# A recommendation network on one core: the first chunk's first cross layer in two halves of two tiles, with three tiles prepared ahead instead of four

## What is computed

```python
target = item_id_feat + item_img_feat
seq_emb = item_table[item_seq]                      # 2048 x 50 rows of 128
x = jnp.concatenate([t, seq_emb, t - seq_emb, t * seq_emb], axis=-1)
scores = (jax.nn.relu(x @ aw1 + ab1) @ aw2 + ab2)[..., 0]
weights = jax.nn.softmax(jnp.where(mask, -1000000000.0, scores), axis=1)
hist_feat = jnp.einsum('bs,bsd->bd', weights, seq_emb)
sparse = jnp.stack([like_feat, view_feat, item_id_feat, item_img_feat, hist_feat], axis=1)
se = sparse * w[:, :, None]                         # w: gate from the means of sparse
p = [vids[:, i] * se[:, j] for i in range(4) for j in range(i + 1, 5)]
dnn_in = jnp.concatenate([se.reshape(B, -1), bil.reshape(B, -1)], axis=1)   # 15 x 128
for i in range(2):
    xc = dnn_in * (xc @ cross_K[i] + cross_bias[i]) + xc
h = jax.nn.gelu(_ln(xc @ w1 + b1, ln1g, ln1b), approximate=False)
h = jax.nn.gelu(_ln(h @ w2 + b2, ln2g, ln2b), approximate=False)
return jax.nn.sigmoid(h @ w3 + b3)[:, 0]
```

## Time and profile before

| | us |
|---|---|
| median of 3 runs | 2186.22 |
| the three runs | 2185.83, 2186.22, 2200.5 |
| the profiled execution, its own time | 2193.55 |
| its span, first to last instruction | 2191.7 |
| mean granted TensorE clock | 0.920 of full speed |

### The profile page before, as it was taken

The page is one execution under the profiler, slowest core; times in us unless marked ns, Lnnn a source line. Parts: engine busy times, 40 slices in busy tenths (PEclk is TensorE's granted clock), DMA queues, the critical chain, the costliest instruction groups (busy, mean ns, idle before and its releaser), DMA issues. The chain is left out here.

```text
span 2191.7 us, 32802 instructions
## 1 busy us (share of the span) xinstructions
PE 1955.1 (89%) x9608; PEld 1534.4 (70%) x9608; DVE 1333.1 (61%) x2213; ACT 902.9 (41%) x1963; POOL 895.4 (41%) x854
## 2 busy tenths in 40 slices
PE   1655653999999999989999999999999999999997
PEld 1433432777777787777777887777777888888885
DVE  3444444567687766566777765667778755445553
ACT  1333333354444434655444434564445333322223
POOL 6666666565565540455555520546551000000000
PEclk6655555999999999999999999999999999999998
DMA  4111111334343463233343452334333352233330
GB/s 155 43 45 45 42 45 41 105 108 121 110 122 99 134 212 91 82 98 103 111 122 114 121 197 80 88 92 120 109 119 98 102 175 84 86 97 100 97 89 20
DMA packets 99535, 220.31 MB, mean 101 GB/s; under 512 B 21648, under 2 KB 27040, under 8 KB 99232
## 3 DMA queue, kind: packets, MB, share of 16 engines
q1 hardware_dynamic: 62928, 136.90, 20.6%
q0 software_dynamic: 27136, 55.63, 10.0%
q10 hardware_dynamic: 9296, 25.70, 3.1%
HBM read 205.29 MB, written 12.85 MB: 100 GB/s over the span
## 5 line engine op out<-in xcount | busy, mean ns | idle before, releaser
L388 POOL DMA_INDIRECT e<-in_item_table,idx_all x800 | 846.5, 1058 | 713.8 <-issue 332.2
L1081 DVE TENSOR_TENSOR Wl<-raw,Wh 128x640 fp32r<-128x640 f32 (+1 forms) x420 | 338.0, 805 | 298.8 <-DVEq L1080 254.7
L765 ACT ACTIVATE Wh<-raw 128x640 fp32r<-128x640 f32 (+1 forms) x420 | 301.7, 722 | 501.2 <-ACTq L764 438.7
L513 PE MATMUL xps<-X0h,Wh 128*128 128x512 f32 x900 | 366.1, 407 | 6.7 <-PEq L511 6.7
L513 PE MATMUL xps<-X1h,Wh 128*128 128x512 f32 x900 | 359.9, 400 | 0.0
L515 PE MATMUL xps<-X0h,Wl 128*128 128x512 f32 x900 | 353.1, 392 | 0.0
L514 PE MATMUL xps<-X0l,Wh 128*128 128x512 f32 x900 | 352.8, 392 | 0.0
L515 PE MATMUL xps<-X1h,Wl 128*128 128x512 f32 x900 | 351.7, 391 | 0.0
L514 PE MATMUL xps<-X1l,Wh 128*128 128x512 f32 x900 | 351.4, 390 | 0.0
L728 ACT ACTIVATE e<-e,pw 128x128 f32<-128x128 f32 x800 | 242.6, 388 | 15.4 <-ACTq L122 10.3
L430 PE MATMUL aps<-ident,e 128*128 128x128 f32 x700 | 113.0, 297 | 102.4 <-issue 83.4
(11 more groups left out here) (144 smaller groups left out, 2240.4 us busy)
## 6 DMA issues: line engine op xcount, KB each, us to landing
raw<-in_cross_K SPq DMA_DIRECT2D x360, 320.0 KB
raw<-in_w SPq DMA_DIRECT2D x60, 256.0 KB
e<-in_item_table,idx_all POOLq DMA_INDIRECT x800
dnn_scratch<-dn ACTq DMA_DIRECT2D x12, 960.0 KB
x1f<-dnn_scratch ACTq DMA_DIRECT2D x3, 2048.0 KB, 9.7
x1f<-dnn_scratch ACTq DMA_DIRECT2D x3, 1792.0 KB
dn<-in_embT SPq DMA_DIRECT2D x1, 1024.0 KB
img_scratch<-dn ACTq DMA_DIRECT2D x1, 1024.0 KB, 5.3
```

Source lines behind the costliest of these rows:

```text
L388: nc.gpsimd.indirect_dma_start(out=dst, out_offset=None, in_=table, in_offset=bass.IndirectOffsetOnAxis(ap=idx_all[:, t, s:s + 1], axis=0) ...
L513: m0 = mm(out, wh, Xh[:, 0:T, k, :], start=(k == 0), stop=False)
L765: af(Wh[:, split_slot(w), 0:n], raw[:, rs, 0:n], ACT.Copy).then_inc(hi_done, 1)
L1081: v.tensor_tensor(Wl[:, rs, 0:n], raw[:, rs, 0:n], Wh[:, slot, 0:n].bitcast(F32), ALU.subtract).then_inc(lo_done, 1)
```

## The change

The first chunk's layer 0 is run twice, once for its tiles 0 and 1 and once for 2 and 3, each time 15 half steps of 256 columns, with layer 0's 45 weight blocks streamed twice. The first half needs tiles 0 and 1 only, so the opening keeps the groups of three tiles (15, 18 steps), and tile 3's groups move under the half steps. In these a group stands in every second step, 15 in all (tiles 3, 4 and 5), its ten transposes come in one run into six places of the transposes' banks and four of the third product bank, which half steps leave, and its later parts are spread over four half steps. Layer 1 of chunk 0 has ten groups (tiles 6 and 7) in its first ten steps, the last in step 24 of 0 to 29. The wait after every five gathers begins at tile 3. Chunks 1 to 3 keep their plan.

```diff
-GROUP_STEPS = {
-    4: [[1 + 6 * j + g for g in range(NG)] for j in range(4)],
...
+EARLY = 2
+EXTRA = FEATS * UNITS
+LEAD = 3
+OPEN_TILES = 3
+OPEN_STEPS = LEAD + NG * OPEN_TILES
+EARLY_AT = OPEN_STEPS
+CHUNK_AT = EARLY_AT + FEATS
...
+    where = [[LEAD + NG * j + g for g in range(NG)] for j in range(OPEN_TILES)]
+
+    where += [[EARLY_AT + 2 * (NG * j + g) for g in range(NG)] for j in range(3)]
+    where += [[CHUNK_AT + FEATS + NG * j + g for g in range(NG)] for j in range(2)]
...
+            if plan[k].half:
+
+                opened = k + 2
+                scored = opened + 1 if plan[opened].half else opened
...
-                        if (s + 1) % (GRP if t < TILES[0] else SUB) == 0:
+                        if (s + 1) % (GRP if t < OPEN_TILES else SUB) == 0:
...
+            def transposes10(t, g, swing):
+                pe.wait_ge(e_landed[g], (t + 1) * (DMA * GRP))
+                pe.wait_ge(tp_free, 1).then_inc(tp_free, -1)
+                for i in range(GRP):
+                    out = tps6[:, i * P:(i + 1) * P] if i < 6 else tps4[:, (i - 6) * P:(i - 5) * P]
+                    last = nc.tensor.transpose(out, e_sub(g, i // SUB, i % SUB), ident[:])
...
+            def half_step(p):
+                products(p, 0)
+                if p.scored:
+                    score()
+                if p.open:
+                    hidden()
+                if p.lift is not None:
+                    tail_turn(p.lift)
+                if p.grp:
+                    transposes10(*p.grp, p.swing is not None)
+                if p.pair is not None:
+                    tail_bilinear()
+
+                products(p, 1)
+                products(p, 2)
+                if p.share is not None:
+                    head_share(p.share)
...
+            def half_step(p):
+                unit(p.first)
+                if p.fetch is not None:
+                    head_fetch(p.fetch)
+                if p.summed:
+                    exps(p.summed[1])
+                    weigh(p.summed[1])
+                unit(p.first + 1)
+                if p.prev:
+                    x_hi(p.prev)
+                unit(p.first + 2)
+                if p.gate is not None:
+                    tail_gate()
+                if p.spread is not None and p.spread < TILES[0]:
+                    tail_hi(p.spread)
+                elif p.spread is not None:
+                    tail_store(p.spread)
+                if p.lift is not None:
+                    tail_copy(p.lift)
+                if p.grp:
+                    copy_eT10(p.swing)
...
+                    if p.spread == TILES[0] - 1:
+                        dve.sem_inc(x_ready, FEATS)
```

More of the change, by code:

```diff
@@ L95, in make_plan @@
-    for c in range(1, CHUNKS):
-        at = open_steps + STEPS * (c - 1)
-        where += [[at + k for k in ks] for ks in GROUP_STEPS[TILES[c]]]
+    plan = [Step(None, k) for k in range(OPEN_STEPS)]
+    plan[-1].last = True
+    for k in range(FEATS):
+        plan.append(Step(0, k, (0, EARLY), k * UNITS))
+        plan[-1].early = True
+    for c in range(CHUNKS):
+        for k in range(STEPS):
+            tiles = (EARLY if c == 0 and k < FEATS else 0, TILES[c])
+            plan.append(Step(c, k, tiles, EXTRA + c * STREAM + k * UNITS))
@@ L98, in make_plan @@
+    for i, p in enumerate(plan[EARLY_AT:EARLY_AT + 2 * FEATS]):
+        p.half, p.bank = True, i % 2
+        p.to_bank2 = i == 2 * (FEATS - 1)
+    for p, q in zip(plan, plan[1:]):
+        if p.chunk is not None and q.chunk == p.chunk:
+            q.prev = p
+    where = group_steps()
+    assert len(where) == sum(TILES)
     for t, ks in enumerate(where):
         for g, k in enumerate(ks):
-            plan[k].grp = plan[k + 1].open = plan[k + 2].summed = (t, g)
-        s, last = ks[0], ks[-1]
@@ L102, in make_plan @@
-        if t < TILES[0]:
+            if plan[k].half:
+                opened = k + 2
+                scored = opened + 1 if plan[opened].half else opened
+            else:
+                opened = scored = k + 1
+                if plan[opened].half:
+                    scored = opened + 1
+                elif plan[opened].chunk is None and not plan[opened].last:
+                    scored = None
+            summed = k + 2 if scored is None else scored + 1
+            plan[k].grp = plan[k + 1 if plan[k].half else k].timed = (t, g)
@@ L627, in step @@
                     transposes(*p.grp, 0)
-                products(p.chunk, p.layer, p.n, 1)
+                products(p, 1)
                 if p.grp:
-                    transposes(*p.grp, 1)
+                    transposes(*p.grp, 1, p.swing is not None)
                 elif p.swing is not None:
@@ L639, in step @@
                     fc_w3(T)
-                products(p.chunk, p.layer, p.n, 2)
+                products(p, 2)
                 if T and 2 <= k < T + 2:
@@ L1207, in step @@
                 if prev:
[L1208 removed]
+                    x_sum(prev)
                 if p.summed:
```

310 lines of the change are left out of this document (200 added, 110 removed).

## The result

The changed kernel takes 2238.39 us (median of 4, 2236.76 to 2238.87), the kernel before 2188.2 us (median of 4, one more run than above): a ratio of 1.0216, 95% interval 1.0189 to 1.0243. It is slower by 1.9 to 2.4%, 48 us above the forecast of 2190 and outside its range. The profiled execution has a span of 2234.6 us against 2191.7.

What follows compares the result with a forecast made beforehand. GpSimd's gathers were taken to bound the first chunk to tile 7's end: 733.6 plus 65.3 us puts w1 at 798.9 instead of 795.30, +3.6 on the 2186.2 median, 2190 us; range 2168 to 2214.

Steps and rivals of the forecast that it cites:

- Step 3: TensorE up to tile 7's last group: half-step pairs of 15.6 us, done at 666, 68 us before the gather.
- the narrow product: Layer 0's 256-column matmuls on TensorE: pitch taken as 0.12 us, bounded by 0.11 and 0.227.
- step 4: VectorE and ScalarE in half steps: below 13 and 10 of 19.2 us; gate chains delay TensorE a few us per tile.
- Step 1: GpSimd's gathers, tiles 3 to 7: 50 sub-groups of five at 9.23 us plus feature triples, ending at 733.6, not 719.7.
- the 14.7: Tile 3's gathers with waits after five: 96.05 us instead of 81.35, +14.7.
- Step 2: From tile 7's last group to the w1 stage: one bare step fewer, 65.3 us, so w1 at 798.9, +3.6.
- Step 5: End of chunk 0: later row store and loads covered by weight blocks three ahead; counted 0, with 4 us as other end.
- The first product: Sign of being right, start of layer 0 on TensorE: near 256 instead of 382.
- C: TensorE falls behind, through narrow products at 0.227 us (2266) or a mean clock of 0.85 (ties with gathers); chance 0.05.
- Rival B: VectorE's two-input instructions lengthen GpSimd's gathers, a fifth of their time; up to 23 us more, 2213; chance 0.13.
- A: The opening's ten steps are really saved: w1 64 us earlier, 2122, or 2155 in part; chance 0.10.

Runs made afterwards that it cites:

- s5: Changed kernel plus idle identity transposes on TensorE ahead of the gate's transposes and the second half's first product; 2249.23 us, ratio 1.0234.
- s7: Changed kernel with VectorE subtracting only 384 of 640 columns of the half steps' weight blocks; half steps 331.8 us against 359.2.
- s6: Changed kernel with five slots instead of four for the weights' high parts, second head matrix kept at half width; half steps 359.6 us against 359.2.
- e3: Changed kernel with gate transposes and exponential later, the hidden layer's maximum and tile 3's pairs earlier on VectorE; 2227.89 us, ratio 1.0126.
- s9: Changed kernel with the edits of s7 and e3, and VectorE summing one row of ten for tiles 3 to 5; half steps 290.7 us.
- b1: Kernel before, waiting after five gathers instead of ten for tile 3 too; tile 4's gathers start 7.9 us later, w1 stage at 804.1.
- b2: Kernel before with one more two-input VectorE instruction ahead of each of layer 0's 45 weight subtractions; layer 0 goes from 211.5 to 225.1 us.

## Why the prediction was wrong, and where it was right

*Where the failure is.* Step 3 had TensorE arrive at tile 7's last group at 666 at the earliest, and put 68 us of slack between that and the gathers at 733.6. It arrived at 778.06: 112 us late, 68 of them covered, 44 not. 843.3 - 798.9 is 44.4. So the forecast had the wrong stream last: the gathers were to bind and TensorE to idle ahead of them, and TensorE came last, with GpSimd waiting for it. What follows tile 7's last group was right to 0.1 us.

*The term.* The pair of half steps: 15.6 us in step 3. From the first group's transposes at 275.93 to layer 1's first at 633.94 it is 358.0 us for 15 pairs, **23.9 each**, tails and the second half's start among them. That is 124 us more than 15 x 15.6; the group steps of layer 1 gave some 16 back against the 160 allowed for them and the tails (144.1 for the nine from 633.94 to 778.06), and the start was 4 late. Of the 124, 88 are TensorE's idle time, the rest is slower work at the granted 0.87 and what step 3 counted under tails; by s5 the slower work cost no time of its own. The part that was doubtful, the narrow product, was right: at full clock they start 0.12 us apart, as in these three rows:

```profile
281.75 0.28 PE L593 MATMUL xps<-X0h,Wh 128*128 128x256 f32 x1
281.87 0.28 PE L594 MATMUL xps<-X0l,Wh 128*128 128x256 f32 x1
281.99 0.28 PE L595 MATMUL xps<-X0h,Wl 128*128 128x256 f32 x1
```

*The step that let it through* is step 4. It put VectorE below 13 us of the 19.2 in which GpSimd delivers a group, and called the rest "a few us once per tile". Three errors are in it. It scaled busy time (10.4 us per step plus three blocks), where a half step also repeats each short instruction with its gap: 14.5 us busy and 3.9 of gaps in a pair, 18.4, which is all but the whole of 19.2. It took an engine at less than the period for harmless, although VectorE works its queue in order and each piece waits for TensorE or ScalarE somewhere. And it priced the chains (8.4 us at each gate, 11.3 and 5.4 at the halves' first products) as stalls that slack pays for, when the ordinary pairs were already longer than the gathers': 20.15 us even at full clock, 275.93 to 296.08. From one group's transposes to the next, ten of the 15 pairs took 20.1 to 23.9 us, 21.4 in the mean, and the five others 25.4 to 32.2; four of these hold a tile's gate or the second half's start. An estimate from these: with 21.4 in all 15, TensorE would have come to tile 7's last group near 741 (275.9 + 321 + 144.1), 7 us behind the gathers; the other 37 came with the five long pairs. s7 is the plainest test of VectorE's part: 24.7 us of subtractions less, 27.4 us less time, in the same order of work. What exactly closes the loop through VectorE's 72 us of longer waits was not singled out; that they are not for want of lead (s6) and only in part for the order (e3) is shown.

*Step 1* was near. In s9, where GpSimd waits for nobody, tile 3 takes 98.57 us beside the weight stream (113 GB/s), against 96.05 in the sum: 9.48 a sub-group. The 40 later ones take 9.27, and tile 7 is through at 737.28 instead of 733.6.

```profile
253.06:351.63 98.57, 76.66 (x548) 68.44 (x547) 57.00 (x110) 48.27 (x110) 56.84 (x53) 0.83 0.40 113
```

b1's +7.9 for the same waits is 8.57 a sub-group without the stream, where the kernel before had 8.54. So its shortfall does not speak against the 14.7. "GpSimd would feel such lag only if a buffer came back late" was right as a condition, and it came to pass: 72.1 us.

*Step 2* was exact for what it sized: 778.06 to 843.29 is 65.23 us, 65.3 predicted.

*Step 5*: the w1 stage takes 44.3 us from its first to its last product against 40.2 before. That is the size of the 4 us named as the other end and counted as 0, but not their cause. The store is issued at 844.85, 1.6 us into the stage as foreseen, the loads at 850.24, and no wait of TensorE follows them. Its one wait in the stage is ahead of them, for a product bank:

```profile
847.88 0.47 PE L624 MATMUL xps<-Wh,X0h 128*128 128x512 f32 x1 [2.14 <-PEq L617]
```

VectorE had tile 7's pairs to do from 842.83 and read the bank only at 846.83. The rest is slower products behind that wait, at a granted 0.96 over the stage.

*The first product* was to come near 256 and came at 268.84, because tile 1's rows are finished only in the last opening step (5.44 us of wait at L591). Group one's transposes were 4 us late for it.

*The rivals.* C was the case that came true, TensorE falls behind, but not by either of its two prices: the pitch is 0.12, and the clock's 0.87 lay above its 0.85 and cost nothing that s5 could show. It should have had a third entry, VectorE. Rival B (gathers lengthened by VectorE) has its piece in b2, some 2 us of longer instructions for 37 us of added work, and is not what happened. A needed 7.9 us per sub-group, and none measured here, with or without the weight stream, had a mean below 8.5. The Trainium skill, "SBUF — State Buffer", section "Who interferes with whom", has two-input VectorE instructions contend with GpSimd instructions that read SBUF; the same section says, as an inference, that making DMA descriptors needs the write side instead, for which such a VectorE instruction does not contend. Of 37 us added in b2 a twentieth shows in the gather instructions, which is nearer to the second; the fifth in rival B had only been read off beside it. The Trainium skill's warning in "TensorE: Matmul & The Clock Gate", section "HAM oscillation — how this bites in real kernels", was borne out as to the pattern (0.80 to 0.83 behind the long waits, 0.90 to 1.00 with the filler) and not as to the time.

No version beats the kernel before. e3 is the best one that computes everything, at 1.0126. Even s9, with work left out, starts its w1 stage 6.5 us later than before, because the gathers of tile 7 end at 737 there.

## What to carry to other kernels

When a step is cut into two, count for every engine the instructions that are repeated, with the gap in front of each, and not the busy time that is moved: VectorE, 64% busy in layer 0 before, came to 96% of the gathers' period that way. Slack pays for a stall only while no other engine is near the same period, as VectorE was here. And to find which engine sets the pace of a loop in which all of them wait, take some 30 us from each in turn; the waits of the trace named TensorE's suppliers, but taking 17 us of those waits away gave 1 us, while 25 to 28 us less work on VectorE gave 20 to 27.

## What the runs showed of the hardware

- Fewer waits for landing made the kernel slower: with one after ten gathers instead of five, a ratio of 1.066 to the kernel before against 1.0216, and matmuls in the middle of a series stood still for 12.0 us in the half steps (2.0 in the change) where nothing in the program holds them. The cause is open.
- Filling TensorE's waits with transposes of the identity lifted the granted clock over the stretches behind them from 0.80 to 0.83 up to 0.90 to 1.00, and the time did not fall with it (165.8 us against 165.5 in the second half).
- VectorE's short instructions cost about as much in gaps as in work: 128x10 elements take 0.16 to 0.23 us, with 0.24 to 0.35 us in front of the softmax's and about 0.15 in front of the gate's. Over the half steps 197 gaps came to 57.8 us beside 219 us of busy time.
- A narrow fp32r product (256 columns, with its weight load) starts 0.12 us after the one before it at the high level of the clock and 0.21 at the low one (269.19, 269.40, 269.62 in the change), against 0.227 for 512 columns at the high one.
